# A graph network kernel: edge-attribute products spread over four column groups of TensorE, and the norm, the overfull picks and layer 0's first two aggregation chunks moved about 20 strips ahead

## What is computed

```python
h = relu(layernorm(x))
for l in range(5):
    edge_emb = edge_attr @ EW[l].T + EB[l]
    agg_x = segment_sum(h[src], dst) + h
    agg_e = segment_sum(edge_emb, dst) + EB[l]
    h = concat(agg_x, agg_e) @ W1[l].T + B1[l]
    h = relu((h - mean(h)) * rsqrt(var(h) + eps) * BNW[l] + BNB[l]) @ W2[l].T + B2[l]
    if l < 4: h = relu(h)
return x + h
```

## Time and profile before

| | us |
|---|---|
| three runs | 639.36, 640.02, 640.08 (median 640.02) |
| the profiled execution, its own time | 638.48 |
| its span, from the first to the last instruction | 636.7 |
| PE busy | 596.7 (94%) |
| DVE busy | 336.3 (53%) |
| ACT busy | 249.9 (39%) |
| POOL busy | 53.3 (8%) |
| mean granted TensorE clock | 0.990 |

### The profile page before, as it was taken

How to read it: one execution, slowest core, us unless ns; L and a number is a source line. 1 busy time by engine, 2 the same in 40 slices (tenths; PEclk the granted TensorE clock), 3 DMA queues, 4 the chain that set the end, 5 groups by cost and what they waited for, 6 DMA issues and landing times.

```text
span 636.7 us, 13078 instructions
## 1 busy us (share of the span) xinstructions
PE 596.7 (94%) x5569; PEld 369.4 (58%) x5569; DVE 336.3 (53%) x708; ACT 249.9 (39%) x544; POOL 53.3 (8%) x59
## 2 busy tenths in 40 slices
PE   6789899879999989999999999999999999999996
PEld 5677677746566644844446644448544458444456
DVE  6999999979899927721214521116411118101126
ACT  0389877646666624601214411116211117011123
POOL 5550224400000000000000000000000000000000
PEclk9899899998999999999999999999999999999999
DMA  5990000000000000000000100000100000100024
GB/s 149 325 296 5 3 4 28 7 7 2 5 5 2 5 4 2 15 19 1 1 1 2 33 1 1 2 1 1 34 1 1 1 2 2 34 1 1 1 72 131
DMA packets 13321, 19.23 MB, mean 30 GB/s; under 512 B 2263, under 2 KB 7397, under 8 KB 13251
## 3 DMA queue, kind: packets, MB, share of 16 engines
q1 hardware_dynamic: 12099, 16.00, 8.3%
q0 software_dynamic: 1152, 2.20, 1.3%
HBM read 16.26 MB, written 1.60 MB: 28 GB/s over the span
## 4 chain that ended last, share of the span: by engine, by line
PE 58%; DVE 3%; ACT 1%; issue 0%; POOLq 0%; DVEq 0%
PE bank L1345 41%; PE bank L1414 9%; PE bank L1381 6%; PE bank L1376 2%; DVE bn_stats L1600 1%; ACT h L1487 1%; DVE bn_small L1606 0%; PE bank L251 0%; ACT bn_small L1483 0%; PE bank L1396 0%; DVE h L1651 0%; PE bank L1332 0%; DVE bound_row L1583 0%; DVE bn_small L1611 0%; DVE bn_small L1613 0%
## 5 line engine op out<-in xcount | busy, mean ns | idle before, releaser
L1345 PE MATMUL bank<-adj,h_pieces 128*128 128x504 bf16 (+1 forms) x1372 | 263.5, 351 | 0.0
L1345 PEld LDWEIGHTS bank<-adj,h_pieces 128*128 128x128 f16 x1372 | 122.9, 97 | 141.4 <-issue 10.2
L1600 DVE BATCH_NORM_STATS2 bn_stats<-bank 128x6 f32<-128x504 f32 (+1 forms) x70 | 42.5, 626 | 216.4 <-PE bank L1381 215.7
L954 ACT ACTIVATE adj<-bank 128x450 bf16<-128x450 f32 x175 | 95.4, 549 | 61.3 <-PE bank L814 57.5
L1468 ACT ACTIVATE h<-bank 128x504 f32<-128x504 f32 (+1 forms) x28 | 15.2, 543 | 226.6 <-PE bank L1345 226.6
L441 DVE TENSOR_TENSOR h<-iota_lo,h 128x1536 bf16<-128x1536 bf16 (+2 forms) x95 | 86.0, 905 | 10.0 <-PE bank L814 7.4
L806 PE MATMUL bank<-h 128*128 128x75 bf16 x1064 | 68.6, 200 | 16.8 <-DVE h L441 16.3
L447 PE MATMUL bank<-adj,h_pieces 128*128 128x450 bf16 x343 | 83.3, 355 | 0.9 <-POOL adj L578 0.9
L806 PEld LDWEIGHTS bank<-h 128*128 128x128 bf16 x1064 | 55.2, 99 | 47.0 <-DVE h L441 25.3
L837 PE MATMUL bank<-h,adj 128*17 128x40 f32 (+11 forms) x1752 | 75.4, 202 | 7.4 <-DVE h L616 5.3
L837 PEld LDWEIGHTS bank<-h,adj 128*17 128x17 f32 x1752 | 65.5, 101 | 12.2 <-DVE h L616 9.9
(11 more groups left out here) (153 smaller groups left out, 365.1 us busy)
## 6 DMA issues: line engine op xcount, KB each, us to landing
adj<-attr SPq DMA_DIRECT2D x1, 2524.5 KB, 22.3
adj<-attr SPq DMA_DIRECT2D x1, 1963.5 KB, 14.6
weights<-wpack SPq DMA_DIRECT2D x5, 323.0 KB
out<-h SPq DMA_DIRECT2D x6, 256.0 KB
adj<-attr SPq DMA_DIRECT2D x1, 1402.5 KB, 6.1
adj<-attr SPq DMA_DIRECT2D x2, 561.0 KB, 5.1
h<-mpack SPq DMA_DIRECT2D x5, 179.0 KB, 2.3
adj<-order SPq DMA_DIRECT2D x2, 202.0 KB, 2.6
```

The costliest lines, as they stand in the source:

```text
L954: nc.scalar.activation(out_view(u), bank_view(n % CNT_BANKS), ACT.Copy).then_inc(s_ev, 1)
L1345: last = nc.tensor.matmul(agg_ps[b][:, 0:w], hp[:, k, s, :], adj[:, k, c * LW:c * LW + w], start=(k == 0 and s == 0), stop=stop and s == p ...
L1600: V.bn_stats(stats[:, h, ds(c * 6, 6)], w1_bank(c, h)).then_inc(st_done, 1)
```

## The change

1. **Column groups.** Edge tile `q` of step `i` writes its product to partitions `32 g` to `32 g + 16`, with `g = (11 i + q) % 4`, where all wrote to partitions 0 to 16. The four partial sums are added by the `stack` product, which now reads 128 rows in place of 17 and has the unit matrices four times in its constants; the copy out of PSUM (L966) has 128 rows too. [...]
2. **Norm sooner.** Three tiles a strip for sums and squares, two for the norm; `SQUARES_AT` from 20 to 16, `SHIFT_AT` from 34 to 27, `NORM_AT` from 36 to 29. The high pieces follow every second strip from 31 to 43 (they came every fourth from 40 to 64), the low pieces on GpSimd with them.
3. **Picks sooner.** `PICK_AT` from 32 to 24, `OV_KEYS_AT` from 45 to 37, and the first two overflow batches from strips 56 and 60 to 42 and 50.
4. **Aggregation.** Chunk 0 is done in strips 49 to 60, chunk 1 in 62 to 73, and chunks 2 to 5 in strips 78 to 100, 103 to 125, 128 to 150 and 153 to 174. Chunks 0 and 1 are copied out at strips 76 and 77, when the attribute work no longer needs the buffer.

The core of the diff:

```diff
-SUMS_AT, SQUARES_AT, SHIFT_AT, NORM_AT = 7, 20, 34, 36
-PICK_AT, OV_KEYS_AT, CHECK_AT = 32, 45, 74
+SUMS_AT, SQUARES_AT, SHIFT_AT, NORM_AT = 7, 16, 27, 29
+PICK_AT, OV_KEYS_AT, CHECK_AT = 24, 37, 74
+MOMENTS, NORMS = 3, 2
-OV_AT = (56, 60, 74, 98, 124, 148, 170)
+OV_AT = (42, 50, 74, 98, 124, 148, 170)
-AGG0_AT, AGG0_SPAN = 68, 106
+AGG0_STRIPS = ((49, 61), (62, 74), (78, 101), (103, 126), (128, 151), (153, STRIPS))
+AGG0_OUT = (76, 77)
...
+def high_unit(u):
+    i, odd = divmod((u - NORM_AT - 2) * NORMS, 4)
+    return i if 0 <= i < UNITS and not odd else None
...
 def agg0_steps(u):
-    n = CHUNKS * NODE_TILES - NODE_TILES
-    return [(j // NODE_TILES, j % NODE_TILES) for j in range(n) if AGG0_AT + j * AGG0_SPAN // n == u]
+    return [(c, k) for c, (a, b) in enumerate(AGG0_STRIPS) for k in range(NODE_TILES) if a + k * (b - a) // NODE_TILES == u]
...
             def stack(w):
-                return nc.tensor.matmul(stack_ps[0:SK, 0:w], cst[0:REC, STACK:STACK + SK], sums[:, 0:w],
+                return nc.tensor.matmul(stack_ps[0:SK, 0:w], cst[:, STACK:STACK + SK], sums[:, 0:w],
...
+                                g = (i * RUN + q) % COL_GROUPS
+                                if c not in begun:
                                     begun.add(c)
                                     if c >= 2:
                                         pe.wait_ge(s_sums, c - 1)
-                                last = nc.tensor.matmul(att_ps[c % 2][0:REC, a - c * CW:b - c * CW],
+                                    nc.tensor.matmul(att_ps[c % 2][:, 0:CW], ident, ident_pad[:, 0:1].to_broadcast([P, CW]),
+                                                     start=True, stop=True, skip_group_check=True)
+                                last = nc.tensor.matmul(att_ps[c % 2][g * GROUP_COLS:g * GROUP_COLS + REC, a - c * CW:b - c * CW],
                                                         attr_i[:, k, t * REC:(t + 1) * REC],
                                                         dst_oh[:, i % DST_SLOTS, q * DW + a - c0:q * DW + b - c0],
-                                                        start=opens, stop=True, skip_group_check=True)
+                                                        start=False, stop=True, skip_group_check=True)
...
-                                nc.scalar.activation(sums, att_ps[c % 2][0:REC, 0:CW], ACT.Copy).then_inc(s_sums, 1)
+                                nc.scalar.activation(sums, att_ps[c % 2][:, 0:CW], ACT.Copy).then_inc(s_sums, 1)
...
+        for g in range(COL_GROUPS):
+            consts[g * GROUP_COLS:g * GROUP_COLS + REC, STACK + t * REC:STACK + (t + 1) * REC] = np.eye(REC)
```

More of the change, by code:

```diff
@@ L88 @@
 PLUS1, S_A, S_B, M_A, M_B, EPSC, ZERO, STACK = 0, 1, 2, 3, 4, 5, 6, 8
+GROUP_COLS = 32
+COL_GROUPS = P // GROUP_COLS
 C_COLS = STACK + SK
@@ L184, in half_at, with ln_tiles, agg0_outs @@
     return HALVES.index((c, h))
-def ln_tiles(u, at):
-    return range(2 * (u - at), min(2 * (u - at) + 2, NODE_TILES)) if at <= u else ()
+def ln_tiles(u, at, n):
+    return range(n * (u - at), min(n * (u - at) + n, NODE_TILES)) if at <= u else ()
+def high_unit(u):
+    i, odd = divmod((u - NORM_AT - 2) * NORMS, 4)
+    return i if 0 <= i < UNITS and not odd else None
 def agg0_steps(u):
-    n = CHUNKS * NODE_TILES - NODE_TILES
-    return [(j // NODE_TILES, j % NODE_TILES) for j in range(n) if AGG0_AT + j * AGG0_SPAN // n == u]
+    return [(c, k) for c, (a, b) in enumerate(AGG0_STRIPS) for k in range(NODE_TILES) if a + k * (b - a) // NODE_TILES == u]
+def agg0_outs(u):
+    late = [c for c, at in enumerate(AGG0_OUT) if at == u]
+    return late + [c for c, k in agg0_steps(u - 1) if k == NODE_TILES - 1 and c >= len(AGG0_OUT)]
 def gin_program(nc, x, first, dst_lin, pair_lin, order, dst_win, src, dst, attr, consts, wpack, mpack, out, rest_dram, starts, picks):
+    assert min(AGG0_OUT) > step_strip(STEPS - 1) + 7
     assert COLS % CHUNKS == 0 and CW % SC == 0 and CHUNKS % 2 == 1 and UNITS % 2 == 1
@@ L302, in gin_program @@
             key_lo = carve(KEYS * 2).rearrange("p (g t) -> p g t", t=2)
-            sums = agg0[0:REC, 0:CW]
+            sums = agg0[:, 0:CW]
             at = CW
@@ L451, in stack, with stack_general @@
             def stack(w):
-                return nc.tensor.matmul(stack_ps[0:SK, 0:w], cst[0:REC, STACK:STACK + SK], sums[:, 0:w],
+                return nc.tensor.matmul(stack_ps[0:SK, 0:w], cst[:, STACK:STACK + SK], sums[:, 0:w],
+                                        start=True, stop=True, skip_group_check=True)
+            def stack_general(w):
+                return nc.tensor.matmul(stack_ps[0:SK, 0:w], cst[0:REC, STACK:STACK + SK], sums[0:REC, 0:w],
                                         start=True, stop=True, skip_group_check=True)
@@ L994, in _ @@
                                                      ).then_inc(s_sd, 1)
-                        k = u - NORM_AT
-                        if 0 <= k < NODE_TILES:
+                        if high_unit(u) is not None:
+                            high_piece(high_unit(u))
+                        for k in ln_tiles(u, NORM_AT, NORMS):
                             if k == 0:
@@ L999, in _ @@
                             normalise(k)
-                        if k >= 4 and k % 4 == 0 and k // 4 <= UNITS:
-                            high_piece(k // 4 - 1)
-                        for c, k in agg0_steps(u - 1):
-                            if k == NODE_TILES - 1:
-                                chunk_out(c)
-                    for c, k in agg0_steps(STRIPS - 1):
-                        if k == NODE_TILES - 1:
+                        for c in agg0_outs(u):
                             chunk_out(c)
+                    for c in agg0_outs(STRIPS):
+                        chunk_out(c)
                     chunk_out(CHUNKS - 1)
@@ L1147, in _ @@
                             pe.wait_ge(s_gev, u + 1)
-                            stack(SC).then_inc(s_gstack, 1)
+                            stack_general(SC).then_inc(s_gstack, 1)
                             pe.wait_ge(s_gpc, 2 * u + 1)
```

16 lines of the change are left out of this document (7 added, 9 removed).

## The result

The changed kernel takes 643.25 us (median of 13 runs, 641.52 to 645.37), the kernel before 640.14 beside it (13 runs). The ratio is **1.0039 [1.0025, 1.0053]**: slower, by 2.5 us (1.6 to 3.4). It leaves out one slow run of the kernel before (654.51 us) and isn't the quotient of the two medians, which lie 3.1 us apart. The forecast was 7.3 us slower. The sign was right, the size three times too large, and the mechanism behind it wrong: rival 3, whose chance was 0.19, describes the column groups.

What follows compares the result with a forecast made beforehand. VectorE was taken to bound strips up to 67, PE strips 78 to 171. Strip 78 comes 13.6 us later, stretch C returns 6.3: +7.3 on the profiled 638.5, 645.8, plus 1.5 for the median, 647.3 us; range 639.0 to 650.5.

Steps and rivals of the forecast that it cites:

- rival 3: All four column groups stream side by side, strips 49 to 73 8.7 us shorter: -1.4 us, 638.6; chance 0.19.
- The body of an attribute step: A strip's 22 attribute matmuls on PE: from 0.77 to 0.66 us, a gain of 0.11 us a step.
- PE's sum in stretch B: Strips 49 to 73: PE becomes the bound, 48.3 us without overlap, 46.2 with it.
- Stretch A: First count to start of strip 49 on PE: VectorE sets the pace, +4.5 us, ends 2 and 6.5.
- The wait for the ranges: VectorE's pick at strip 24 may wait 0.5 to 1 us for the ranges; set to zero.
- Stretch C: Strips 78 to 171: VectorE gives the pace, 71.6 us against 77.9, so -6.3 us.
- Rival 1: The column groups don't overlap at all in the attribute steps: +9.4 us, 649.4; chance 0.22.
- Rival 2: Starts in another group nearly free, a product's two halves still follow each other: +2.5 us, 642.5; chance 0.16.
- Rival 4: Chunk 0's gate at strip 49 is late through GpSimd's pieces, PE waits 3 us or more: 650.5; chance 0.05.
- Wrong if L837 x22 is under 0.5: Test for strips 49 to 60: the 22 attribute matmuls take 0.85 us; under 0.5 the forecast is wrong.

Runs made afterwards that it cites:

- e2: The changed kernel with all attribute products in one column group, everything else as changed: 656.33 us, ratio 1.0233 to the kernel before.
- e4: The changed kernel with chunk 1's aggregation spread over strips 62 to 77, copied out at 78: 639.31 us, ratio 0.9974 to the kernel before.
- e7: The changed kernel with chunk 0 in strips 49 to 62 and chunk 1 in 63 to 77: 639.77 us, ratio 0.998 to the kernel before.
- e11: The changed kernel with GpSimd's low pieces cut from 128 to 8 columns, the high piece aggregated twice: ratio 1.0009 to the kernel before.
- e3: The changed kernel plus idle matmuls on PE, 18 in strip 75 and 9 in strip 77: 641.21 us, ratio 0.9998 to the kernel before.
- e1: The kernel before with the column groups alone, its schedule untouched: 638.67 us, ratio 0.9957 to the kernel before.
- e6: The changed kernel with one column group and the old aggregation from strip 68, leaving only the moves: 644.05 us, ratio 1.004 to the kernel before.
- e12: The changed kernel with chunk 1 spread to strip 77, the pick at strip 27 and first overflow batch at 46: 638.66 us, ratio 0.9960 to before.
- e15: The kernel before with TensorE held up once, by 12 idle matmuls at strip 31: 640.06 us, ratio 0.9991 to the kernel before.

## Why the prediction was wrong, step by step

**The body of an attribute step** is the step that failed. "So about 25 ns is the least between any two starts" was read from the earlier trace rows, and every matmul of those rows writes to one and the same column group: they bound what one group can do and say nothing of two. I knew that the trace had no such pair, and still took the end that the rows lay nearest to. The body fell from 0.77 to 0.20 us, not to 0.66: 19 x 0.46 = 8.7 us (e2: 10.7 from 49 to 78, where 2.1 were forecast).

**PE's sum in stretch B** was otherwise right: 57.2 reckoned without overlap, 57.56 measured in e2. PE is busy without a pause from strip 49 to 68 in the profiles of the changed kernel, e2, e4 and e7. From the end of strip 73 to strip 78 it took 8.7 us (142.57 to 151.31) where 8.9 were reckoned.

**Stretch A**, +4.5, measured +4.58, is right by luck. VectorE's terms are there (low pieces, overflow batch), but taking the low pieces away gave 1.9 of the 4.5. The norm was costed only by its squares; that ScalarE normalises two tiles a strip in place of one (1.46 us a strip against 1.24) was left out, and it holds the stretch by itself (e11). It leans on the faster attribute steps too, which the forecast didn't have: with one group (a body of 0.77 us, where 0.66 was forecast) e2's profile starts strip 49 8.6 us later than before. The wait for the ranges, 0.5 to 1 us that the prediction set to zero, was none in the one profile of the changed kernel, and 0.87 to 2.95 in eight of its nine relatives with the pick at strip 24.

**Stretch C** was taken too large: 71.6 forecast, 75.5 measured. The pace came out as said (a batch every 1.41 us, for 1.43, with VectorE in front), and an overflow batch costs 1.26 to 1.46 more than a plain step (1.1 said). Two things were not in the sum: the lower clock behind TensorE's idle time at strips 74 to 78, which makes the batches of strips 82 and 84 later by 1.35 and 0.84 (e3 takes most of it away and gains 1.9 in the stretch), and eight steps of 1.54 to 1.69 us, 1.5 in all, six of them where a chunk begins. A and B came out nearly as rival 3 has them (strip 78 at 151.3 for 150.8), so C, 3.9 us, is nearly the whole reason that it came out 2.5 us slower and not 1.4 faster.

**The rivals.** Rival 1, no overlap, is e2 in effect, and was 7 us too low (649.4, measured 656.3): in e2's profile stretch A is 4.1 and stretch C 4.3 us longer than in its sum. Rival 2 had the short gap nearly right (6 to 8 ns, not 4) and the two halves of a product wrong: no gap of 35 ns is left between any two starts of the step. Rival 3 was right on its mechanism and, by 4.6 us of time, not on the sum. Rival 4, a late gate, didn't occur: PE is never idle in strips 49 to 67. "Wrong if L837 x22 is under 0.5": it is 0.40.

**What of the change pays**: the column groups (e1, 0.9957). The moves alone cost 2.6 us (e6). The whole change costs as much (1.0039), so the early aggregation takes about what the groups give, 2.7 us if the three parts simply add up; no kernel here has the groups and the moves without it. With aggregation, pick and overflow batch repaired (e12, 0.9960) the whole comes out level with e1. No kernel here beats the groups alone, and the smallest edit is as fast as any.

## What to carry to other kernels

Where the trace lacks the very pair that a change creates (two matmuls in different column groups), rows of the nearest kind bound nothing beyond their own kind; give the far end a real chance, or price it by geometry. When work is packed more tightly, add up every engine for one strip of the new schedule, not only the one that bounds the old; two nearly full engines hide each other, and only relieving both shows it. And look where a now faster TensorE will stand idle: it may come back at the lower clock just where it begins to bound again (1.7 us in e1, 1.9 in the changed kernel). A hold-up put in as a test belongs where the engine doesn't wait soon after in any case (e15).

## What was unexpected of the hardware

- Starts of f32 matmuls (128 x 17 stationary, 40 columns) 6 to 8 ns apart with four column groups; 22 of them in a slot of 0.33 us in place of 0.90.
- After idle times of 4.12 and 2.30 us TensorE ran at its 1.2 GHz level from strip 78 (151.31) to 155.7 us: four matmuls of 450 columns took 1.66 us in place of 0.92.
- With the column groups, stretch A has a granted clock of 0.67 in place of 0.96 and is no longer for it (e1: 79.8 us, before 80.2); the price, 1.7 us, comes behind it, in strips 68 to 73.
- VectorE beside a GpSimd instruction on f32 and f16 pieces: 1.21 us for 128x256 in place of 0.28, or GpSimd 8.27 us for three pieces while VectorE loses little. In e11, where GpSimd touches 32 columns, VectorE's largest loss beside a piece is about 0.2 us (1.30 for two window one-hots).
